# Attention one tile earlier, no filler matmuls, and a turned gate product in a fused two-layer block

## The reference, cut to what matters

```python
# x: (2, 2048, 512) f32, ctx: (2, 128, 512)
q = relu(layernorm(x) @ Wq + bq); k = relu(ctx @ Wk + bk); v = relu(ctx @ Wv + bv)
x = x + relu((relu(q @ k.T) / sqrt(512) + mask) @ v)             # attention, first residual
x = x + fp6_blocks(layernorm(x)) @ fp6_blocks(Wf).T + bf         # blocks of 32, second residual
x = x + layernorm(x) @ W1.T + mean(ctx) @ W2.T + b               # mix, third residual
logits = layernorm(x) @ Wg + bg                                  # 16 experts
# per batch and expert: softmax over tokens, the 128 best tokens go through
# relu(t@w1+b1), relu(.@w2+b2), .@w3+b3, weighted by their probability, added to x
```

## Time and profile before

| what | us |
|---|---|
| median of 3 runs | 799.23 (798.38 to 800.33) |
| the profiled execution | 801.92, its span 799.9 |
| turn 1: ffn(0) ends, TensorE waits 1.60 for the first norm of tile 10 | 56.2 to 57.8 |
| granted TensorE clock from 61.0 to 68.6 | 0.58 of full |
| turn 1: last weight group, ScalarE's two copies (L844) start | 70.92 |
| turn 1: VectorE's two low parts end, mean_rows starts | 72.85, 73.55 |
| turn 2: TensorE starts t3(0); mix(0) starts | 77.08; 87.71 |
| turn 2: gate_shift (L682) starts, VectorE copies its result (L1138) | 84.48, 86.38 |
| turn 3, turns 4 to 6, turn 7 (start to start of t3) | 13.63, 3 x 10.55, 14.38 |
| turns 28, 29, 30, 31, 32 | 9.60, 9.60, 9.62, 11.65, 7.56 |
| VectorE's lo3 ends in turn 33, mix(31) starts | 431.17, 431.22 |
| phase 2, TensorE, 500 to 700 | busy 200.0 of 200.0 |

### The profile page before, as it was taken

The page is one execution under the profiler, slowest core; times in us unless marked ns, Lnnn a source line. Parts: engine busy times, 40 slices in busy tenths (PEclk is TensorE's granted clock), DMA queues, the critical chain, the costliest instruction groups (busy, mean ns, idle before and its releaser), DMA issues.

```text
span 799.9 us, 12388 instructions
## 1 busy us (share of the span) xinstructions
PE 706.4 (88%) x4400; PEld 628.2 (79%) x4400; DVE 576.3 (72%) x1016; ACT 377.5 (47%) x553; POOL 432.3 (54%) x589
## 2 busy tenths in 40 slices
PE   6989999999999999998887004999999999999994
PEld 6767888888888888887776003999999999999993
DVE  5785789798888978777784986476776667667751
ACT  5753354444544544333222301566556665666540
POOL 2734788887888888776663503033344433333331
PEclk9998999999999999999999556999999999999998
DMA  9610122222212221111112424387788888887642
GB/s 310 223 27 14 39 79 81 68 80 81 77 58 94 66 72 64 55 53 42 53 55 79 160 79 150 97 237 232 214 237 245 242 238 240 234 248 212 194 86 37
DMA packets 54093, 103.05 MB, mean 129 GB/s; under 512 B 5392, under 2 KB 6672, under 8 KB 54032
## 3 DMA queue, kind: packets, MB, share of 16 engines
q1 hardware_dynamic: 46864, 85.47, 32.9%
q0 software_dynamic: 7168, 16.78, 9.4%
HBM read 76.68 MB, written 25.17 MB: 127 GB/s over the span
## 4 chain that ended last, share of the span: by engine, by line
PE 69%; DVE 16%; POOL 6%; issue 4%; DMA 2%; ACT 1%; SPq 1%; POOLq 0%; DVEq 0%; ACTq 0%
PE bank L249 39%; PE banks L249 11%; PE bank L256 5%; PE banks L555 4%; PE banks L561 4%; DVE bn L1096 2%; PE banks L565 2%; PE banks L566 2%; DVE x L1272 1%; DVE pack L1356 1%; POOL xd L1591 1%; DVE left L1363 1%; DVE pos L1358 1%; DVE q L1301 1%; DMA stage<-wq 1%
## 5 line engine op out<-in xcount | busy, mean ns | idle before, releaser
L1630 POOL DMA_INDIRECT out<-y,ids x32 | 76.2, 2380 | 173.8 <-DVE y L1476 169.2
L1108 DVE TENSOR_TENSOR w_l<-w_raw,w_h 128x2048 fp32r<-128x2048 f32 x45 | 103.1, 2290 | 31.4 <-ACT w_h L844 31.4
L1059 ACT ACTIVATE h<-bank,b 128x512 f32<-128x512 f32 x64 | 44.0, 688 | 107.5 <-PE bank L249 107.5
L1096 DVE BATCH_NORM_STATS2 bn<-x 128x6 f32<-128x512 f32 x128 | 88.2, 689 | 8.2 <-DMA x<-x 4.9
L844 ACT ACTIVATE w_h<-w_raw 128x2048 fp32r<-128x2048 f32 x48 | 90.7, 1927 | 4.9 <-DMA w_raw<-w 4.9
L1108 DVE TENSOR_TENSOR hT_l<-h,hT_h 128x512 fp32r<-128x512 f32 x64 | 44.2, 691 | 67.1 <-ACT hT_h L1065 67.1
L249 PE MATMUL bank<-tokT_l,w_h 128*128 128x256 f32 x256 | 72.4, 283 | 0.0
L249 PE MATMUL bank<-tokT_h,w_l 128*128 128x256 f32 x256 | 72.4, 283 | 0.0
L249 PE MATMUL bank<-hT_h,w_h 128*128 128x256 f32 x256 | 72.4, 283 | 0.0
L249 PE MATMUL bank<-hT_h,w_l 128*128 128x256 f32 x256 | 72.4, 283 | 0.0
L249 PE MATMUL bank<-tokT_h,w_h 128*128 128x256 f32 x256 | 72.4, 283 | 0.0
(11 more groups left out here) (241 smaller groups left out, 2181.8 us busy)
## 6 DMA issues: line engine op xcount, KB each, us to landing
w_raw<-w SPq DMA_DIRECT2D x48, 1024.0 KB, 6.2
x<-x SPq DMA_DIRECT2D x32, 256.0 KB, 2.8
out<-x SPq DMA_DIRECT2D x32, 256.0 KB, 2.1
xn<-xn SPq DMA_DIRECT2D x32, 256.0 KB, 2.0
mask<-mask_t SPq DMA_DIRECT2D x8, 256.0 KB, 3.2
stage<-wk SPq DMA_DIRECT2D x1, 1024.0 KB, 8.1
stage<-wq SPq DMA_DIRECT2D x2, 512.0 KB, 8.9
stage<-wf SPq DMA_DIRECT2D x1, 1024.0 KB, 11.7
```

Source lines behind the costliest of these rows:

```text
L1059: act.activation(h32[n % 2][:, :], ps_hid[n % 4][:, :], ACT.Relu, bias=bias)
L1096: dve.bn_stats(bn6[which][:, j % 2, :], src[:, :]).then_inc(sem_bn[which], 1)
L1108: dve.tensor_tensor(dst, src, hi_part, ALU.subtract).then_inc(sem, 1)
L1630: pool.indirect_dma_start(out=out_rows, out_offset=bass.IndirectOffsetOnAxis(ap=ids[:, r:r + 1], axis=0), in_=y[e % 2][b][:, :], in_offset ...
```

## The change

- **Attention and first residual.** In turns without scores attend(k+1) is issued before t2(k), and VectorE does the first residual of tile k+1, with its statistics, right after the second residual of tile k-1, in front of the statistics of tile k+10, the logit parts and lo2(k). In turns with scores attend(k+1) moves behind mix(k-2), and the first residual stays behind lo2(k).
- **Fillers.** All are gone but one group: four in turn 33, before mix(31).
- **Gate product.** The gate's 16 columns are stationary and the weight moves, 4 matmuls of 512 columns in place of 16 of 16 columns; ScalarE copies the [16, 512] result out ("gt"), and four small transposes (`mix_gate_turned`), after the q chunk, turn it. t1(10), and with it hi1(10) and lo1(10), stand behind it.
- **GpSimd.** The second factor of the fourth norm raises a semaphore of its own (`g_b4`), and `g_r4` is raised one instruction earlier.

```diff
         def mix_gate():
+            for o in range(C):
+                last = pe.matmul(ps_ta[0:E, :], wgf[:, o, 0:E], stage[0][:, o, :], start=(o == 0), stop=(o == C - 1))
+            last.then_inc(sm.p_set, 1)
+        def mix_gate_turned():
+            pe.wait_ge(sm.a_set, A["gt"])
             for c in range(C):
-                for o in range(C):
-                    last = pe.matmul(ps_ta[:, c * E:(c + 1) * E], stage[0][:, o, c * P:(c + 1) * P],
-                                     wgf[:, o, 0:E], start=(o == 0), stop=(o == C - 1))
+                last = pe.transpose(ps_ta[:, c * E:(c + 1) * E], gate_t[:, c * P:(c + 1) * P], ident[0:E, 0:E])
             last.then_inc(sm.p_set, 1)
...
-            if valid(k + 9):
-                t1(k + 9)
             if k == 1:
                 mix_weights(0)
                 mix_weights(1)
                 mix_gate()
+            if valid(k + 9):
+                t1(k + 9)
...
-            elif valid(k - 2):
-                pe.wait_ge(sm.a_q, N)
-                keep_warm(3 if valid(k) else 6, wq_h, ps_q[0])
+            if k == 1:
+                mix_gate_turned()
             if k == 2:
                 mean_row(0)
                 gate_shift()
+            if valid(k + 1) and scores_of(k) is None:
+                attend(k + 1)
             if valid(k):
                 t2(k)
-            if valid(k + 1):
-                attend(k + 1)
...
             if valid(k - 2):
+                if k == LAST - 2:
+                    pe.wait_ge(sm.a_q, N)
+                    keep_warm(4, wq_h, ps_q[0])
                 mix(k - 2)
+            if valid(k + 1) and scores_of(k) is not None:
+                attend(k + 1)
...
+            if k == 1:
+                setup("wc0")
+                setup("wc1")
+                q_relu(*q_of(4))
+                setup("gt")
             j = k + 9
             if valid(j) and k >= 1:
                 hi1(j)
...
+        def ahead(k):
+            return k >= 1 and scores_of(k) is None
+        first_residual(0)
         for k in range(LAST + 1):
...
             if k == 1:
+                lo1(10)
                 setup("v1")
                 setup("w1g")
+            if ahead(k) and valid(k + 1):
+                first_residual(k + 1)
             g = scores_of(k)
...
                 lo(sm.d_lo2, xd_l[:, :, :], in4(ps_tb), xd_h[:, :, :])
+            if not ahead(k) and valid(k + 1):
+                first_residual(k + 1)
```

More of the change, by code:

```diff
@@ L69, in build @@
         a_xn1 a_xc a_xn4 a_hi1 a_hi2 a_hi3 a_q a_s a_l a_seg
-        g_r1 g_r2 g_r3 g_r4 g_x1b g_xd g_qlo g_x2b s_lo
+        g_r1 g_r2 g_r3 g_r4 g_b4 g_x1b g_xd g_qlo g_x2b s_lo
         k_top k_cand k_sum k_exp k_tr k_out k_pos a_soft
@@ L180, in build @@
     junk = place("mix_w_scaled", [P, C, D], at=at_ab + 4 * KB)
+    gate_t = place("mix_gate_rows", [E, D], at=at_x2 + 14 * KB)
     crow = place("mix_mean_rows", [B, D], at=at_x2 + 12 * KB)
@@ L313, in counts @@
         return at
-    A = counts("wq0 wq1 k0 k1 k2 k3 wsum v0 wf0 wf1 wf2 wf3 wcn v1 wc0 wc1 wc2 wc3 crow row0 row1")
+    A = counts("wq0 wq1 k0 k1 k2 k3 wsum v0 wf0 wf1 wf2 wf3 wcn v1 wc0 wc1 gt wc2 wc3 crow row0 row1")
     V = counts("wgc wq0 wq1 wf8 va0 v0 wf0 wf1 wf2 wf3 va1 mean wc0 wc1 v1 w1g wc2 wc3 cbcol cg")
-    T = counts("wgm k0 k1 k2 k3 v0 wf0 wf1 wf2 wf3 v1 wc0 wc1 w1g wc2 wc3 crow col row0 cg row1")
+    T = counts("wgm k0 k1 k2 k3 v0 wf0 wf1 wf2 wf3 v1 wc0 wc1 gt w1g wc2 wc3 crow col row0 cg row1")
     GS = counts("half mean k01 k23 wf")
@@ L882, in setup @@
                 last.then_inc(sm.a_set, 1)
+            if what == "gt":
+                act.wait_ge(sm.p_set, T["gt"])
+                hi(sm.a_set, gate_t[:, :], ps_ta[0:E, :])
             if what == "crow":
@@ L982, in _ @@
                 hi1(j)
-            if k == 1:
-                setup("wc0")
-                setup("wc1")
             j = k - 3
@@ L989, in _ @@
                     act.wait_ge(sem_xn4[j % 2], 16 * (j // 2))
-                norm(3, j, x3[j % 2], xn4[j % 2], sm.a_xn4, sm.g_r4)
+                norm(3, j, x3[j % 2], xn4[j % 2], sm.a_xn4, sm.g_b4)
             g = scores_of(k)
@@ L993, in _ @@
                 s_relu(g)
-            if k == 1:
-                q_relu(*q_of(4))
             if q_units(k):
@@ L1251, in logit_scale, with first_residual @@
                               r_all[1][:, four].unsqueeze(2).to_broadcast([P, GRP, E]), ALU.mult).then_inc(sm.d_lg, 1)
-        for k in range(LAST + 1):
-            j = k
-            if valid(j):
-                dve.wait_ge(sm.p_av, j + 1)
-                dve.wait_ge(sem_x[j % XR], 16 * (j // XR + 1))
-                dve.scalar_tensor_tensor(x1[j % 2][:, :], ps_av[:, :], 0.0, x_in[j % XR][:, :], ALU.max, ALU.add)\
-                    .then_inc(sm.d_x1, 1)
-            if valid(k):
-                dve.wait_ge(sm.d_x1, k + 1)
-                stats(1, k, x1[k % 2], sm.d_st2)
+        def first_residual(j):
+            dve.wait_ge(sm.p_av, j + 1)
+            dve.wait_ge(sem_x[j % XR], 16 * (j // XR + 1))
+            dve.scalar_tensor_tensor(x1[j % 2][:, :], ps_av[:, :], 0.0, x_in[j % XR][:, :], ALU.max, ALU.add)\
+                .then_inc(sm.d_x1, 1)
+            dve.wait_ge(sm.d_x1, j + 1)
+            stats(1, j, x1[j % 2], sm.d_st2)
+        def ahead(k):
+            return k >= 1 and scores_of(k) is None
+        first_residual(0)
+        for k in range(LAST + 1):
             j = k - 3
@@ L1315, in _ @@
             j = k + 9
-            if valid(j) and k >= 1:
+            if valid(j) and k >= 2:
                 lo1(j)
@@ L1515, in rstd_of @@
                 return
-            inverse = r_all[1][:, j:j + 1] if which == 3 else r[:, 1:2]
-            then(pool.tensor_tensor(inverse, r[:, 0:1], eps_exp[:, :], ALU.pow))
+            if which == 3:
+                inverse = r_all[1][:, j:j + 1]
+                pool.tensor_tensor(inverse, r[:, 0:1], eps_exp[:, :], ALU.pow).then_inc(sem, 1)
+                pool.wait_ge(sem, j + 1)
+                pool.tensor_scalar(r[:, 2:3], m[:, 0:1], inverse, -1.0, ALU.mult, ALU.mult).then_inc(sm.g_b4, 1)
+                return
+            then(pool.tensor_tensor(r[:, 1:2], r[:, 0:1], eps_exp[:, :], ALU.pow))
             if which == 1:
@@ L1520, in rstd_of @@
             else:
-                pool.tensor_scalar(r[:, 2:3], m[:, 0:1], inverse, -1.0, ALU.mult, ALU.mult).then_inc(sem, 1)
+                pool.tensor_scalar(r[:, 2:3], m[:, 0:1], r[:, 1:2], -1.0, ALU.mult, ALU.mult).then_inc(sem, 1)
         def lo(sem, dst, src, hi_part):
```

## The result

| | median us | runs | profiled execution | its span |
|---|---|---|---|---|
| before | 799.68 | 4 (798.38 to 800.33) | 801.92 | 799.9 |
| after | 808.74 | 4 (808.65 to 813.16) | 808.77 | 806.9 |

The changed kernel is slower: ratio 1.0129, 95% interval [1.0092, 1.0166] (it weighs all executions, also the one of 813.16; the ratio of the medians is 1.0113). The forecast was 798.4, from 795.0 to 801.4. The two profiled executions differ by 7.0 in span, the medians by 9.1; the profiled execution of before was itself 2.2 above its median. All 7.0 are there when turn 33 begins (428.70 before, 435.70 after); behind it the kernels run alike.

A forecast was written before the change was run, and what follows sets the result against it. TensorE, 88% busy, was taken to bound the kernel, so the change is worth its effect on TensorE's idle time in phase 1. +2.4 - 4.8 - 1.7 + 1.6 + 0 + 1.7 = -0.8 gave 798.4 us, range 795.0 to 801.4.

The forecast's parts named there:

- setup up to t3(0): Setup and turn 1: the gate product costs equal time, 1.8 is gained at mean_rows and given back in turn 2; net 0.
- turn 2: End of setup: +1.7 us, from a clock fall after 2.6 idle before mean_rows, or zero if the clock holds.
- turns 3 to 26: Steady turns: the gain of the score turns is eaten, +0.54 a group of four turns, +2.4 us in all.
- turn 27: Scores turn without q matmuls: mix follows t2 at once and the attention ends the turn at 11.06; -4.8 us.
- turn 28: First drain turn: +1.1 us for the late residual and +1.6 for a clock fall after 3.3 idle.
- turns 29 to 31: Drain: turns 29 and 30 give -0.8 us each as the attention leaves the ring; turn 31 +0.1.
- turn 32: Drain: without the six fillers between ffn and mix, mix starts 1.36 us earlier.
- Turns without scores: Turns 8 to 10: VectorE's and GpSimd's queues get longer; turns of 10.73, 11.35 and 10.54, lo2 wait 0.57 in turn 11.
- The third rival: GpSimd's lateness does not end in turn 9: 0.6 us more in every turn 10, five times, 801.4; chance 0.15.
- The first wait: Setup: TensorE idles 2.6 us before mean_rows, which starts at 71.7, and the clock falls.
- Turn 2 gives it back: Turn 2: the gate shift is copied at 87.7, mix(0) starts at 87.8 after 2.1 idle; the 1.8 gained is lost.
- the first rival: The clock holds where a fall was forecast: 796.7 us if at turn 1, 795.1 if at turn 28 as well; chance 0.27.

The follow-up runs named there:

- bias_one_input: Changed kernel with GpSimd's mix bias as an addition of constant zero to x2, in its place, the bias left out: 805.04 us (one execution).
- bias_late: Changed kernel with GpSimd's mix bias moved from ahead of the rstd of x3 to after the bias of x1: 799.05 us, ratio 0.9980.
- bias_half: Changed kernel with the mix bias on 256 of the 512 columns only, in its place: 803.85 us (one execution).
- from_turn_3: Changed kernel, but in turns 1 and 2 the attention comes after t2 and the residual at the turn's end, as before: 803.29 us, ratio 1.0046.
- drain_only: Kernel before with, from turn 24, attention and residual moved as in the change, and no fillers but four in turn 33: 792.94 us, ratio 0.9916.
- stats_first: Changed kernel with the statistics of input tile k+10 put ahead of the next tile's residual on VectorE: 794.87 us, ratio 0.9945.
- bias_and_scores: Kernel before with new gate product, drain_only's changes, attention after mix in scores turns from turn 7, mix bias after the bias of x1: 791.36 us, ratio 0.9898.
- bias_by_turn: bias_and_scores with fillers ahead of t2 in turns 28 and 31, and the mix bias in its old place in scores turns: 788.59 us, ratio 0.9842.

## Why the prediction was wrong

By its own steps, in span against the profiled execution of before (forecast, measured):

| step | forecast | after |
|---|---|---|
| setup up to t3(0) | 0 | -0.2 |
| turn 2 | +1.7 | +3.8 |
| turns 3 to 26 | +2.4 | +12.4 |
| turn 27 | -4.8 | -5.0 |
| turn 28 | +2.7 | +1.15 |
| turns 29 to 31 | -1.5 | -3.7 |
| turn 32 | -1.36 | -1.4 |
| sum | -0.8 (rounded terms) | +7.0 |

**Turns without scores** is the step that failed. Turn 8 was right (10.73, 10.77), turn 9 nearly (11.35, 11.52). The failing sentence is "Turn 10: GpSimd starts at 1.73, xd ends at 7.04, no wait". In the prediction's own terms, GpSimd's first rstd starts, from the turn's start, at 1.92, 2.54 and 1.73 in turns 8, 9 and 10. Measured were 1.92, 2.66 and 2.66. From turn 9 to 10 the forecast has 1.73 + 11.35 - 2.54 = 10.54 between the two, and 11.51 was measured. Of these 0.97, 0.84 is xs: 1.19 in place of the 0.35 of the earlier trace rows's turn, since VectorE now waits for GpSimd's rstd and xs starts beside the mix bias from that step's beginning. So a lateness that was to end in turn 9 is renewed each turn. Turn 10 came out 0.98 longer, the scores turn 0.82: by then the input statistics are so late that ffn, held by lo2, starts 1.74 after t3, 1.39 late and not 0.57. This is 2.0 for a group, and 10 for five groups. The rest of the ring was right: without the hold-up it is 10.54 to 10.56.

The third rival had the mechanism ("GpSimd's lateness does not end in turn 9") and its point of decision, 0.02 from the value taken. Its price of 0.6 in each turn 10 was the wait of turn 9; measured were 0.98 and the longer scores turn. A rival so near to its own threshold deserved more than 0.15, and its price had to be worked out with VectorE late.

**Setup.** The first wait was right: mean_rows at 71.67 (forecast 71.7), at half clock, which cost 1.7 (5.29 against 3.59). The same wait of 2.58 ended without a fall in bias_one_input, so it was in part luck that the fall came. "Turn 2 gives it back" was right as well: the copy of the gate shift came at 89.34, the forecast's 87.7 and its +1.7. The residual starts only at 86.99, when the attention has left TensorE, and residual, two statistics and their last steps (2.35) stand ahead of the copy. What failed is the price of the second wait: 1.92 long, it was named and put at nothing, and behind it the clock fell (mix(0) to the end of the turn 4.60 against 3.07, 1.5). In bias_late, bias_half and bias_one_input the same wait of 1.92 brought no fall, and turn 2 took 15.92 to 15.96. from_turn_3, without the residual ahead, has 13.70 for turn 2, and starts it 3.0 earlier.

**Drain.** Turns 27, 29, 30 and 32 were right to 0.3. In turn 28 the clock did not fall in this execution, as the first rival had it, and the +1.1 for the late residual was right (1.15); turn 31 gained 2.25 where +0.1 was forecast, as the clock stayed up (9.40, against 10.93 in drain_only: 1.5) and the logit step (L1263, before L1250) beside the mix bias took 0.52 and no longer 1.23 (0.7).

**The start.** The prediction subtracted 0.8 from the median of 799.23, but worked against an execution 2.7 above it, with a fall of the clock in its setup that not every profile has (t3(0) at 77.08, in drain_only 74.13). This choice of base accounts for the 2.5 us between the miss of 7.8 in span and that of 10.3 in median.

What stays open: whether a fall comes in a given execution can't be told from the order; why one GpSimd step with one input lets VectorE in before its end; and why one or two of the three turns keep 10.8 instead of 10.55 once the ring is open (bias_late, stats_first).

## What to carry to other kernels

Before moving a step into an engine's queue, close the ring: follow what each engine waits for until you are back at the same step one turn later, and add up that sum, not the busy time. A duration read from the trace holds for its neighbours of that trace; when a move makes an engine wait for another, its next step starts beside that engine's next step, and if both are VectorE and GpSimd, price the collision. A change of several parts should be tried part by part: here two parts were together worth 8 to 9 us, the rest, by difference, lost 18, and in the steady turns there was nothing to gain to begin with.

## What the runs showed of the hardware

- A VectorE step of 16 columns takes as long as the two-input GpSimd step beside it has left: 1.19, 0.63 and 0.23 us with a neighbour of 1.29, 0.74 and none. Beside a one-input step of 1.51 it mostly took 0.51. GpSimd loses as well: its mix bias took 1.77 beside VectorE's addition of the mask (bias_and_scores, turn 11), 1.29 elsewhere.
- Not every VectorE step is held up: in turn 10 of before the statistics of x3 (L1096) and the block maxima (L1286) ran beside the mix bias in 0.69 and 0.67, their usual lengths.
- The same idle time can end in a fall of the clock or not. Six kernels have one of 3.2 ahead of t2 in turn 28, ended by xd; in four of the profiles the clock fell behind it, in two not. In the changed kernel the transpose behind it took 0.66, at 2.4 GHz (granted 1.00):

```profile
398.84 0.66 PE L257 MATMUL bank<-ident,xd 128*128 128x128 f32 x4 [3.21 <-POOL xd L1619]
```

and in drain_only 1.12, at 1.2 GHz (granted 0.50):

```profile
379.72 1.12 PE L257 MATMUL bank<-ident,xd 128*128 128x128 f32 x4 [3.20 <-POOL xd L1610]
```

The turn then took 10.75 and 13.32. The waits of 2.58 and 1.92 in the setup went either way too. So one profile does not give the price of an idle time, only what it can be. The executions of drain_only lie between 791.62 and 797.20; the mean granted clock is 0.957 in the three shortest and 0.949 in the longest. Thirteen filler matmuls in two idle times took turn 28 from 12.11 to 10.55 and, over four executions each, the spread from 2.1 us to 0.8; bias_by_turn has the same fillers and a spread of 2.5 over five, so that the narrower spread is not shown to be theirs.
